# Node rows in the layers of a graph network: eight consecutive rows in a partition, as one 4096-byte piece

## What is computed

```
edge_index = stack([src, dst])
h = relu(layernorm(x))                                     # layer 0: SAGE, mean over the edges into a node
summed = segment_sum(h[src], dst);  deg = segment_sum(1, dst)
x = x + (summed / max(deg, 1)) @ W_l.T + h @ W_r.T
h = relu(layernorm(x))                                     # layer 1
agg = segment_sum(edge_attr, src)
h = concat([h, agg]) @ W1 + b1;  h = batchnorm(silu(h), g1, be1)
h = h @ W2 + b2;                 h = batchnorm(silu(h), g2, be2)
x = x + h @ W3 + b3
```

## Time and profile before

| | before |
| --- | --- |
| median of 3 runs | 1426.01 us (1422.4 to 1430.45) |
| span of the profiled execution | 1425.6 us |
| TensorE matmul / weight load busy | 1038.0 us (73%) / 744.8 us (52%) |
| VectorE busy | 1066.8 us (75%) |
| ScalarE busy | 860.6 us (60%) |
| GpSimd busy | 881.3 us (62%) |
| packets, bytes moved by DMA | 202877, 315.38 MB, 221 GB/s in the mean |

### The profile page before, as it was taken

The page is one execution under the profiler, slowest core; times in us unless marked ns, Lnnn a source line. Parts: engine busy times, 40 slices in busy tenths (PEclk is TensorE's granted clock), DMA queues, the critical chain, the costliest instruction groups (busy, mean ns, idle before and its releaser), DMA issues.

```text
span 1425.6 us, 22736 instructions
## 1 busy us (share of the span) xinstructions
PE 1038.0 (73%) x5520; PEld 744.8 (52%) x5520; DVE 1066.8 (75%) x4684; ACT 860.6 (60%) x1688; POOL 881.3 (62%) x625
## 2 busy tenths in 40 slices
PE   0027766776766666665988898887878889999875
PEld 0015545555555445453565565555545766447765
DVE  2119888888886667666999899898874888787756
ACT  0017767776766555552777777876775556669610
POOL 7757888888888888876777777776761000002433
PEclk9989999999999888988999999999998999999999
DMA  9967888877776666657898999988978995216999
GB/s 331 371 253 170 212 213 209 223 160 173 164 163 142 152 146 137 137 136 186 208 237 222 234 239 225 236 213 218 231 198 270 363 333 183 88 59 228 406 408 369
DMA packets 202877, 315.38 MB, mean 221 GB/s; under 512 B 20913, under 2 KB 72535, under 8 KB 202785
## 3 DMA queue, kind: packets, MB, share of 16 engines
q1 hardware_dynamic: 135000, 266.54, 54.9%
q0 software_dynamic: 62720, 38.57, 22.4%
q10 hardware_dynamic: 5064, 9.29, 1.9%
HBM read 163.49 MB, written 150.84 MB: 220 GB/s over the span
## 4 chain that ended last, share of the span: by engine, by line
POOL 37%; DMA 28%; issue 18%; PE 11%; SPq 3%; DVE 2%; ACT 1%; another core or an unknown queue 0%; POOLq 0%; DVEq 0%; ACTq 0%
POOL acc L899 21%; POOL acc L919 9%; DMA acc<-tabs,target_b 8%; DMA acc<-zT,target_b 7%; DMA zT<-x_dram 7%; POOL xin L877 6%; PE ps L1740 6%; DMA xin<-acc 2%; DMA acc<-zT,tabs 1%; PE ps L1704 1%; PE ps L1707 1%; SPq L618 1%; PE ps L1710 1%; DMA res<-acc 1%; DMA zT<-z_dram 1%
## 5 line engine op out<-in xcount | busy, mean ns | idle before, releaser
L1601 PE MATMUL ps<-zT 128*128 128x512 f32 (+5 forms) x784 | 262.4, 483 | 167.1 <-ACT zT L1038 121.6
L899 POOL DMA_INDIRECT acc<-zT,tabs x196 | 316.8, 1616 | 82.2 <-issue 62.1
L1601 PEld LDWEIGHTS ps<-zT 128*128 128x128 f32 (+1 forms) x784 | 158.7, 209 | 294.4 <-issue 198.3
L919 POOL DMA_INDIRECT acc<-zT,target_b x100 | 157.2, 1572 | 56.2 <-issue 24.8
L1354 DVE BATCH_NORM_STATS2 zT<-zT 128x6 f32<-128x128 f32 (+1 forms) x384 | 79.4, 277 | 146.9 <-DMA zT<-in_x_dram 134.2
L919 POOL DMA_INDIRECT acc<-tabs,target_b x96 | 151.0, 1573 | 54.3 <-issue 25.2
L877 POOL DMA_INDIRECT xin<-in_x_dram,tabs x140 | 141.7, 1012 | 42.6 <-issue 41.7
L1593 PE MATMUL ps<-ident,zT 128*128 128x128 f32 (+1 forms) x784 | 113.3, 292 | 43.4 <-ACT zT L990 39.3
L998 ACT ACTIVATE hT<-ps 128x1024 f32<-128x1024 f32 (+1 forms) x100 | 99.8, 1000 | 43.7 <-PE ps L1593 23.6
L1593 PEld LDWEIGHTS ps<-ident,zT 128*128 128x128 f32 (+1 forms) x784 | 94.1, 152 | 57.3 <-ACT zT L990 48.8
L1479 DVE BATCH_NORM_STATS2 bst<-zT (+1 forms) x168 | 107.3, 683 | 18.5 <-ACT zT L1141 17.4
(11 more groups left out here) (201 smaller groups left out, 2279.7 us busy)
## 6 DMA issues: line engine op xcount, KB each, us to landing
acc<-bst SPq DMA_DIRECT2D x12, 2112.0 KB
acc<-bst SPq DMA_DIRECT2D x48, 528.0 KB
zT<-in_x_dram SPq DMA_DIRECT2D x48, 512.0 KB
zT<-acc SPq DMA_DIRECT2D x48, 512.0 KB
zT<-x_dram SPq DMA_DIRECT2D x42, 512.0 KB, 10.0
out_dram<-zT SPq DMA_DIRECT2D x42, 512.0 KB, 10.6
zT<-row_dram SPq DMA_DIRECT2D x49, 256.0 KB
zT<-in_edge_attr_dram SPq DMA_DIRECT2D x48, 256.0 KB
```

The source lines that it names most:

```text
L899: pool.indirect_dma_start(acc1, bass.IndirectOffsetOnAxis(ap=target_a[:, k, j:j + 1], axis=0), v[:, j, :], None, compute_op=ALU.add).then_ ...
L919: pool.indirect_dma_start(acc2, bass.IndirectOffsetOnAxis(ap=target_b[:, k, j:j + 1], axis=0), vrow_b[k % RING][:, j, :], None, compute_op ...
L1601: ins = nc.tensor.matmul(psA[:, 0:j + 1, 0:p], t[0:p, j, :], same[0:p, par, at:at + j + 1, 0:p], start=(j == ROWS - 1), stop=(j == 0))
```

## The change

A round is now laid out with eight consecutive rows in each partition: partition p holds the rows 8p to 8p + 7, one contiguous piece of 4096 bytes in memory. All node tensors (x, y, x1, the output and both accumulators; eight loads and stores in each round that spills) are read and written with the new views. The tail of 848 rows becomes 106 partitions with 8 rows each, in one DMA instead of two. The name of the partition within a round is now bits 3 to 9 of the node's number (bits 2 to 8 before), that of the chunk its lowest 3 bits, and the semaphore counts of the tail fall by one DMA. The diff, cut to its core:

```diff
@@ -62,10 +62,10 @@
...
-    NODE_TAIL = [P, (N - RF * ROUND - GROUP) // ROWS]
+    NODE_TAIL = (N - RF * ROUND) // CHUNKS
...
-    assert RF % 2 == 0 and E // GROUP == RF and GROUP + NODE_TAIL[1] * ROWS == N - RF * ROUND
-    assert EDGE_TAIL * ROWS == E - RF * GROUP and 0 < EDGE_TAIL <= P and 0 < NODE_TAIL[1] <= P
+    assert RF % 2 == 0 and E // GROUP == RF and NODE_TAIL * CHUNKS == N - RF * ROUND
+    assert EDGE_TAIL * ROWS == E - RF * GROUP and 0 < EDGE_TAIL <= P and 0 < NODE_TAIL <= P
...
@@ -95,10 +95,8 @@
...
-        full = t[0:RF * ROUND, :].rearrange("(r n p j) d -> r p n (j d)", n=2, p=P, j=ROWS)
-        a = t[RF * ROUND:RF * ROUND + GROUP, :].rearrange("(p j) d -> p (j d)", j=ROWS)
-        b = t[RF * ROUND + GROUP:N, :].rearrange("(p j) d -> p (j d)", j=ROWS)
-        return full, (a, b)
+        return (t[0:RF * ROUND, :].rearrange("(r p j) d -> r p (j d)", p=P, j=CHUNKS),
+                t[RF * ROUND:N, :].rearrange("(p j) d -> p (j d)", j=CHUNKS))
...
@@ -293,13 +291,15 @@
...
+        def node_parts(tail):
+            return NODE_TAIL if tail else P
...
-            return [(slice(0, ROWS), NODE_TAIL[0]), (slice(ROWS, CHUNKS), NODE_TAIL[1])] if tail else \
-                [(slice(0, CHUNKS), P)]
+            return [(slice(0, CHUNKS), node_parts(tail))]
...
-            return [(c, NODE_TAIL[c // ROWS] if tail else P) for c in range(CHUNKS)]
+            return [(c, node_parts(tail)) for c in range(CHUNKS)]
...
@@ -370,10 +370,8 @@
...
-            if tail:
-                return [(slice(0, ROWS), NODE_TAIL[0]), (slice(ROWS, DVE_C), NODE_TAIL[1])], \
-                    (slice(DVE_C, CHUNKS), NODE_TAIL[1])
-            return [(slice(0, DVE_C), P)], (slice(DVE_C, CHUNKS), P)
+            p = node_parts(tail)
+            return [(slice(0, DVE_C), p)], (slice(DVE_C, CHUNKS), p)
...
@@ -521,7 +519,7 @@
...
-                return 16 * (i // 2 + (2 if tail else 1))
+                return 16 * (i // 2 + 1)
...
@@ -560,20 +558,12 @@
...
-                for n in range(2 if tail else 0):
-                    p = NODE_TAIL[n]
-                    sp.dma_start(t[0:p, n * ROWS:(n + 1) * ROWS, :].rearrange("p j d -> p (j d)"),
-                                 v[1][n]).then_inc(sem, 16)
-                if not tail:
-                    sp.dma_start(t.rearrange("p (n j) d -> p n (j d)", n=2), v[0][r]).then_inc(sem, 16)
+                p = node_parts(tail)
+                sp.dma_start(t[0:p, :, :].rearrange("p c d -> p (c d)"), v[1] if tail else v[0][r]).then_inc(sem, 16)
...
-                for n in range(2 if tail else 0):
-                    p = NODE_TAIL[n]
-                    sp.dma_start(v[1][n], t[0:p, n * ROWS:(n + 1) * ROWS, :].rearrange("p j d -> p (j d)"))\
-                        .then_inc(sem, 16)
-                if not tail:
-                    sp.dma_start(v[0][r], t.rearrange("p (n j) d -> p n (j d)", n=2)).then_inc(sem, 16)
+                p = node_parts(tail)
+                sp.dma_start(v[1] if tail else v[0][r], t[0:p, :, :].rearrange("p c d -> p (c d)")).then_inc(sem, 16)
...
@@ -610,7 +600,7 @@
...
-                sp.wait_ge(sems[0], 16 * (IT - kept_its + 2))
+                sp.wait_ge(sems[0], 16 * (IT - kept_its + 1))
...
@@ -1197,12 +1187,12 @@
...
-            link(nc.vector.tensor_scalar(ints[:, 0, :], raw, 2, P - 1, ALU.logical_shift_right, ALU.bitwise_and))
+            link(nc.vector.tensor_scalar(ints[:, 0, :], raw, 3, P - 1, ALU.logical_shift_right, ALU.bitwise_and))
...
-            link(nc.vector.tensor_scalar(ints[:, 1, :], raw, 9, None, ALU.logical_shift_right))
-            link(nc.vector.tensor_scalar(ints[:, 0, :], raw, ROWS - 1, None, ALU.bitwise_and))
+            link(nc.vector.tensor_scalar(ints[:, 1, :], raw, 10, None, ALU.logical_shift_right))
+            link(nc.vector.tensor_scalar(ints[:, 0, :], raw, CHUNKS - 1, None, ALU.bitwise_and))
...
-                dst_tab[:, :, 3, :], ints[:, 1, :].rearrange("p (r j) -> p r j", j=ROWS), float(ROWS),
+                dst_tab[:, :, 3, :], ints[:, 1, :].rearrange("p (r j) -> p r j", j=ROWS), float(CHUNKS),
...
@@ -1418,8 +1408,8 @@
...
-                    dve.wait_ge(B["y_loaded"][par], (node[0] - KEPT + 1) * 16 + (16 if tail else 0))
-                dve.wait_ge(*((B["a_loaded"][0], 16 * (IT + 2)) if tail else this(B["a_loaded"], par, i, 16)))
+                    dve.wait_ge(B["y_loaded"][par], (node[0] - KEPT + 1) * 16)
+                dve.wait_ge(*this(B["a_loaded"], par, i, 16))
...
@@ -1672,7 +1662,7 @@
...
-                    q = NODE_TAIL[n] if tail else P
+                    q = node_parts(tail)
...
```

More of the change, by code:

```diff
@@ L382, in late @@
         def late(i, par, tail, times):
-            return late_loaded[2 * (i - KEPT_LATER) + par], 32 * (times + 1) if tail else 16 * times
+            return late_loaded[2 * (i - KEPT_LATER) + par], 16 * (times + 1) if tail else 16 * times
         def late_times(i):
@@ L844, in _ @@
             sp.wait_ge(G["stored"][1], 16 * (IT - EARLY_G))
-            sp.wait_ge(G["stored"][0], 16 * (IT - EARLY_G + 2))
+            sp.wait_ge(G["stored"][0], 16 * (IT - EARLY_G + 1))
         @block.gpsimd
@@ L1350, in body_a @@
                 p = edge_parts(tail)
-                dve.wait_ge(*((A["x_loaded"][0], 16 * (IT + 2)) if tail else this(A["x_loaded"], par, i, 16)))
+                dve.wait_ge(*this(A["x_loaded"], par, i, 16))
                 x_t = rows_a(i, par, tail, late)
@@ L1476, in count_batch @@
                 for half in range(2):
-                    p = NODE_TAIL[half] if tail else P
+                    p = node_parts(tail)
                     c = slice(half * ROWS, (half + 1) * ROWS)
@@ L1548, in finish @@
                 else:
-                    dve.wait_ge(x1_loaded[odd][par], 16 * (half + (2 if tail else 1)))
+                    dve.wait_ge(x1_loaded[odd][par], 16 * (half + 1))
                     chain["at"], chain["n"] = done[0] + i, 0
```

## The result

| | before | after |
| --- | --- | --- |
| median of the timed runs | 1425.17 us (4 runs, 1422.4 to 1430.45) | 1477.63 us (4 runs, 1475.51 to 1484.31) |
| ratio of the medians, 95% interval | | 1.0357 (1.0314 to 1.04): slower |
| profiled execution: time, span | span 1425.6 us | 1484.31 us, span 1482.6 us |
| packets, bytes | 202877, 315.38 MB | 161580, 315.38 MB |

The changed kernel is 52 us slower.

What follows compares the result with a forecast made beforehand. It took the DMA engines to limit G and half of C, GpSimd to pace A and TensorE to limit F. Terms 8 - 2 + 10 + 5 + 10 = +31 us gave 1457 us, range 1432 to 1480.

Steps and rivals of the forecast that it cites:

- The last round on two engines: Last round's eight node transfers: 106 partitions use two engines, 8.6 us alone each, 7.4 us more than before.
- rival 1: The last round spreads over the engines all the same, leaving only the pieces' gain: 1417 us, faster; chance 8%.
- End of B, +10 us: End of B, start of C: last y and aggregate loads and x1 store delay C's first loads, +10 us (6 to 16).
- C, +7 us: Sweep C: the load behind the last aggregate load waits 7.4 us longer for two engines; +7 us (2 to 9), net +5.
- G, +14.8 us: Sweep G: last x1 load and last store in line on the same two engines, twice 7.4 us (10 to 18), net +10.
- End of A, start of B, +8 us: Late last x load, then B's opening aggregate loads behind a long y store: +8 us (3 to 12).
- Pieces, -9 us: 4096-byte pieces instead of two of 2048 are cheaper: -4.7 us in G, -2 in C, -2 in B.
- Fewer instructions, nothing: Last round: two activations, additions and DMA issues become one in a few places; costed at nothing.
- the second: Rival: the long transfers are covered except in G; 1432 us, no measurable change; chance 9%.
- The third: Rival: scatters in B land 0.6 us later in each of 48 rounds, +29 on top, 1486 us; chance 6%.
- The fourth: Rival: the compiler cuts pieces back to 2048 bytes, so only the last round's loss remains: 1466 us; no chance given.

Runs made afterwards that it cites:

- the uncut kernels: Kernels with the new layout whose last-round node transfers of sweep B stay single DMAs of 106 partitions, the changed kernel (1477.63 us) among them.
- C uncut: Kernels with the new layout whose last aggregate load of sweep C stays one DMA of 106 partitions; that load takes 15.04 to 16.04 us.
- G cut: Changed kernel with only sweep G's last x1 load and last output store each cut into DMAs of 96 and 10 partitions: 1465.98 us, ratio 1.0241.
- A uncut: Kernels with the new layout whose last x load and y store of sweep A stay single DMAs of 106 partitions, the changed kernel (1477.63 us) among them.
- all transfers cut: Changed kernel with all eight last-round node transfers cut into DMAs of 96 and 10 partitions: 1429.78 us, ratio to the kernel before 1.000.
- the four cuts: Changed kernel with the last round's node transfers cut into 96 and 10 partitions in only sweep A, B, C or G: 1461.86, 1458.81, 1467.75, 1465.98 us.

## Why the prediction was right and where it was short

The direction and the mechanism held, and the time is inside the range; the forecast of +31 us fell 21 us short. The terms below show that the total came inside the range although two of its largest parts (the start of B and the pieces) were mis-sized, both towards too fast, and one (G) towards too slow. Term by term:

- **The last round on two engines: right.** 12.8% of 16 engines after the last store, 6.4% with 53 partitions, and no loss with 96 and 10. The Trainium skill (DMA: Bandwidth & Descriptors, Why a DMA increments its semaphore by 16 and not by 1) has the count as the largest up to 16 that divides the outermost one, which is 2 for 106 and 1 for 53: the traces agree with both. The durations were right too: 53 pieces of 150 to 161 ns. One piece of evidence was misread: that the queue "never occupies more than two engines" in the 12 us of the edge load. From 1043.5 to 1048 us it took 90.9% of 16 engines with earlier transfers; only from 1049.5 us on the 11.6% show what was left, and 53 pieces of 96 ns are 5 of the 12.6 us. It was the runs that settled rival 1, not these rows.
- **End of B, +10 us: right.** 48.3 us in the mean of the uncut kernels, 36.4 in those cut, a difference of 12. The working has a slip: its own terms from 1055.7 (1.3, 9.2, 1.3, 9.2) give 1076.7, not 1077.7.
- **C, +7 us: right.** The load at the end of the chain is 6.5 us longer, the whole of C 8.3 us in the means (132.7 to 136.4 us in five kernels with C uncut, 124.8 to 129.0 in four with it cut). Two of the 7 us were to be given back by the pieces, and were not, see below.
- **G, +14.8 us: too much.** The sweeps F and G are 10.7 us shorter with G cut. The step "Both are in line on the same two engines: twice 7.4" holds for the store, 12.8 - 4.2 = 8.6 us. From the issue of the last x1 load to that of the store are 17.0 us in the change and 13.8 with G cut, so the load costs about 3: before, GpSimd and VectorE needed that time for their last full round anyway, and only the remainder of the load comes on top. The bounds of the net term (7 and 16) also don't follow from those of its parts, 10 to 18 and -6 to +3, which give 4 and 21; the range would have been 1435 to 1485 us.
- **End of A, start of B, +8 us: the term that failed most.** It measured 14, outside its range of 3 to 12. The prediction had the x load move the round by about 8 us and then treated the y store as a delay of the aggregate loads in its place (671 instead of 663). It left their issue at 659.06 and let the last scatter of A absorb the delay. But SyncE issues them only when that scatter has landed, and in the kernels with A uncut it starts 5.2 us later, behind work that waited for x, and lands 5.7 us later, beside the long store: 11 us before the loads are issued. In the same queue stand the loads of the next rounds' edges: the one of the third round lands after 12.68 us, TensorE's products wait for it, and with them the scatters (693.6 against 680.8). So the work behind a delayed and long store had been costed for one transfer, the aggregate load, and not for the scatter that releases it and the edge loads beside it.
- **Pieces, -9 us: only -2.5 came**, in G. The step that failed is from engine time to the length of the sweep. The price of a large piece was right (161.4 ns measured, 162.6 read), yet the rate rose by 2 to 3% and not by the 4.2% of the price; the 424 GB/s of the earlier trace rows come from a stretch of 4 us. The Trainium skill (DMA: Bandwidth & Descriptors, Why small descriptors are slow) gives 2.2% by its overhead per packet, an estimate, and the -2.5 us that the prediction set beside its own sum is what was measured. In C and B nothing was gained; that the landings waited for there would shorten with the pieces was argued, and no run bears it out.
- **Fewer instructions, nothing: not contradicted.** With all transfers cut, the kernel has these savings but for the DMA issues, and the ratio is 1.000.

In sum 14 + 12 + 8.3 + 10.7 - 2.5 = 43 us, of 52 measured. Of the rest, about 5 us may be the stretch of B, if it is more than noise; the other 4 are within what one profile differs from a median here (6.7 us in the change, 10.8 us in the kernel with all cut), and no place for them was found.

Of the rivals, the first (the round spreads anyway) and the second (covered except in G) fall with the share of 12.8% and with the four cuts, each of which gained. The third (each round's scatter lands 0.6 us later, +29) falls with GpSimd's waits; a sixth of its size could hide in the open 5 us. What the runs do show is another effect on a scatter: one beside a transfer on two engines lands 5.7 us late. The fourth falls with the packets, 161580 instead of 202877.

No kernel here beats the one before; the best with the new layout equals it.

## What to carry to other kernels

When a tile of a partial round is laid out anew, look at its number of partitions before its number of DMAs: 106 partitions in one transfer ran on two of 16 engines, 53 on one, and 96 + 10 in two transfers on enough that all of 51 us came back. Where such a transfer is moved or made larger, follow everything that is issued behind it, on its own queue and on GpSimd's, up to the first reader that somebody waits for, and do so once for each long transfer, since a load and the store that depends on it add up. And larger pieces were worth 2 to 3% only in the sweep in which the DMA engines are the limit, so price them by the share of the kernel in which they are, and by the rate, not by the time that a piece holds its engine.

## What was not expected of the hardware

A scatter that GpSimd issues, in another queue than SyncE's, is late beside a store on two engines: the last scatter of A took 8.8 to 9.8 us until it released SyncE in the five kernels with that store, 3.2 to 3.8 us in the nine without. The same holds for a load that itself spreads well: the edge load issued 0.7 us behind the y store landed after 12.68 us. Two DMAs of 53 partitions, issued one right after the other, used the same single engine rather than one each (6.4% of 16 engines, 20.5 us); that was not in the prediction, though expected before its run. Making the edge load of 106 partitions land earlier (its reader ran 6.1 us behind the issue instead of 8.8 to 12.6) brought nothing (0.9984, 0.9955 to 1.0013), though in the profile TensorE had waited 2.77 us for it.
